# One layer's running maximum spread with 128-row operands, and one list sum moved between two products

## The chip, the core and the metric

The kernel runs on one core of a Trainium2 chip. Its metric is the device time of one execution in microseconds (us); a lower time is better. Below, TensorE is the matrix engine (PE in the rows, PEld for its weight loads), VectorE is DVE, ScalarE is ACT, GpSimd is POOL and SyncE is SP. In the rows TensorE's granted clock is a fraction of full speed: 1.00 is the level of 2.4 GHz, 0.50 that of 1.2 GHz.

## What is computed

Eight sequences of 512 tokens with 256 features, in float32, go through two layers. Cut to what matters:

```
x = x + mlstm(layernorm(x), ctx, ctx)      # 4 heads; decay matrix D = exp(log_D - running max), normalised
x = x + mlp(layernorm(x))                  # 256 -> 1024 -> 256, gelu
x = x + attention(layernorm(x), ctx, ctx)  # 16 heads of 64, softmax
x = x + moe(layernorm(x))                  # 8 experts, 512 places each; h = gelu(x w1.T), y = h w2.T, weighted
```

In the mLSTM each row of the decay matrix is `exp(g[key] - max over keys so far of g)`, where `g` is the input gate less the summed log of the forget gate. In the experts' layer each expert takes its best 512 tokens of those routed to it, and its results, weighted, are added into the output.

## The kernel before, in words

The work is written as a row of stages; inside a stage each engine has its own program, in an order written out by hand, and semaphores join them.

**Gates.** Tokens and context are loaded, normalised and turned, and the gates of all 32 pairs of head and sequence come out as 32 rows of 512. VectorE's program begins with `memset` of the gate weights and two copies that fill `pick` (L308 to L310), then waits for the first tokens (L311). At the end it splits the running maximum `gmax` into a high and a low part and writes them to `ghl`, rows 0 to 31 and 32 to 63 (L353, L354). `pick` has 64 rows of 32 columns: the unit matrix twice.

**Mixer and MLP** (`mix_and_mlp`). A step `b` runs from -2 to 8 and does the mixer of sequence `b + 2`, the MLP of sequence `b`, and the turns between them. For each head `spread_max` (L465) multiplies a column of `pick`, broadcast to 128 columns, with `ghl`: every partition of the result in PSUM then holds the running maximum of that head, 512 columns wide. ScalarE makes `Dm = exp(...)` of it (L576). The other products of TensorE in a step are `states` (L475), `spread_decay` (L483, 64 rows), `scores` (L492, 64 rows), `values` (L504, L507), `turn` (L434), `hidden` (L446) and `mapped` (L456). In the steps -2 and -1 there is no MLP yet.

**Attention** and the **router** follow; the change touches neither.

**Experts** (`experts`). For each expert VectorE builds a one-hot table and the numbers to be summed (`build`, L1588 to L1603), TensorE sums them (`sum_numbers`, L1517, 32 small matmuls), and VectorE turns the sums into the lists of rows to fetch and to write (`read`, L1613 to L1621; the list to fetch is `idx_get`, L1618). GpSimd then issues four indirect transfers that gather the expert's tokens (`gather`, L1483), and later four that add the results into the output (`put`, L1494). GpSimd's order is: gathers of experts 0, 1 and 2; then for each expert its puts and the gathers of the expert three further on. TensorE's order for each expert is: turn the tokens (L1528), first product in two halves `f = 0` and `f = 1` (L1536), the list sum of the expert two further on, second product (L1546). ScalarE applies gelu to each half (L1579); VectorE scales the results into `y` (L1637), and after expert `e` builds and reads the list of expert `e + 3`.

```
                for e in range(AHEAD):
                    build(e)
                    read(e)
                for e in range(E):
                    scale(e)
                    if there(e + AHEAD):
                        build(e + AHEAD)
                        read(e + AHEAD)
```

Of the kernel before, what the change touches and what calls it, by code (L numbers as in the profile page):

```python
# [11 lines left out]
F32 = mybir.dt.float32  # L12
F32R = mybir.dt.float32r
# [3 lines left out]
ALU = mybir.AluOpType  # L17
# [4 lines left out]
P = 128  # L22
B, S, D = 8, 512, 256
# [3 lines left out]
DC = D // P  # L27
MH, MD = 4, 64
# [13 lines left out]
KINDS = 2 * TPB + 6  # L42
# [124 lines left out]
def mlstm_gates(nc, c, x, x_all, xnT_all, ctxT_all, g, ctx_in, ig_kernel, ig_bias, fg_kernel, fg_bias, prefetch):  # L167

    R = MH * B
    WIDE = 2 * R + R - MH  # L170
    RING = 4
    with ExitStack() as ctx:
# [10 lines left out]
        ps = ctx.enter_context(nc.psum_tensor("mg_ps", [P, 8, 512], F32))  # L183
# [5 lines left out]
        ident = c["ident"]  # L189

        with nc.Block() as block:
# [114 lines left out]
            @block.vector  # L306
            def _(dve):
                dve.memset(gate_w[:, :, :], 0.0).then_inc(s["gw"], 1)  # L308
                dve.tensor_copy(g["pick"][0:R, :], ident[0:R, 0:R])
                dve.tensor_copy(g["pick"][R:2 * R, :], ident[R:2 * R, R:2 * R])  # L310
                dve.wait_ge(s["x0"], 16)  # L311
                norm_stats_dve(dve, s, 0, x_all, tmp[0])
                dve.wait_ge(s["gw"], 1)
                dve.wait_ge(s["w"], 16 * 2)
                for half in range(2):
                    src = gk_in[:, :, MH * half:MH * half + MH]
                    at = R - MH + R * half
                    dst = gate_w[:, :, at:at + MH]
                    dve.tensor_copy(dst[:, 0:DC, :], src[:, 0:DC, :]).then_inc(s["gw"], 1)

                    dve.tensor_tensor(dst[:, DC:2 * DC, :], src[:, DC:2 * DC, :], src[:, 2 * DC:3 * DC, :],
                                      ALU.add).then_inc(s["gw"], 1)
                for i in range(B):
                    if i + 1 < B:
                        dve.wait_ge(s[f"x{(i + 1) % RING}"], 16 * ((i + 1) // RING + 1))
                        if i:
                            wait_apart(dve, s["xn"], i)
                        norm_stats_dve(dve, s, i + 1, x_all, tmp[(i + 1) % 2])
                    norm_apply_dve(dve, s, i, x_all, tmp[i % 2],
                                   lambda: dve.wait_ge(s["xn_turned"], i - 1) if i > 1 else None)  # L330

                def row(ins, k):
                    ins.then_inc(s["rows"], 1)
                    dve.wait_ge(s["rows"], k)

                dve.wait_ge(s["fg"], 1)
                dve.tensor_tensor(fg[:, :], ps[3 * R:4 * R, GATE_BANK, :], fg[:, :], ALU.add).then_inc(s["summed"], 1)
                dve.wait_ge(s["summed"], 1)
                row(dve.scalar_tensor_tensor(out=absf[:, :], in0=fg[:, :], scalar=-1.0, in1=fg[:, :],
                                             op0=ALU.mult, op1=ALU.max), 1)  # L340
                dve.wait_ge(s["act_rows"], 2)
                row(dve.scalar_tensor_tensor(out=fg[:, :], in0=fg[:, :], scalar=0.0, in1=lfg[:, :],
                                             op0=ALU.min, op1=ALU.subtract), 2)
                row(dve.tensor_tensor_scan(cums[:, :], c["ones_row"][0:R, :], fg[:, :], 0.0, ALU.mult, ALU.add), 3)
                dve.wait_ge(s["ig"], 1)
                dve.tensor_tensor(ig[:, :], ps[2 * R:3 * R, GATE_BANK, :], ig[:, :], ALU.add).then_inc(s["summed"], 1)
                dve.wait_ge(s["summed"], 2)
                row(dve.tensor_tensor(gg[:, :], ig[:, :], cums[:, :], ALU.subtract), 4)
                row(dve.tensor_tensor_scan(gmax[:, :], gg[:, :], gg[:, :], -3.0e38, ALU.max, ALU.max), 5)
                row(dve.tensor_scalar(neg_r[:, :], gmax[:, :].rearrange("r (t p) -> r t p", p=P)[:, :, P - 1],  # L350
                                      -1.0, None, ALU.mult), 6)
                row(dve.tensor_tensor(logmax[:, :], cums[:, :], gmax[:, :], ALU.add), 7)
                row(dve.tensor_copy(g["ghl"][0:R, :], gmax[:, :]), 8)  # L353
                row(dve.tensor_tensor(g["ghl"][R:2 * R, :], gmax[:, :], g["ghl"][0:R, :], ALU.subtract), 9)  # L354
                dve.wait_ge(s["act_rows"], 6)
                row(dve.tensor_copy(g["bhl"][0:R, :], bb[:, 0:S - P]), 10)
                row(dve.tensor_tensor(g["bhl"][R:2 * R, :], bb[:, 0:S - P], g["bhl"][0:R, :], ALU.subtract), 11)
                dve.wait_ge(s["cols_ps"], 1)
                dve.tensor_copy(g["cols"][:, :, :], ps[:, COL_BANK, 0:KINDS * R].rearrange("p (k r) -> p k r", r=R)
                                ).then_inc(s["cols"], 1)  # L360
# [17 lines left out]
def mix_and_mlp(nc, c, g, x_all, xnT_all, ctxT_all, ctx_in, early, prefetch):  # L378

    R = MH * B  # L380
# [5 lines left out]
    with ExitStack() as ctx:  # L386
# [17 lines left out]
        H_BANK, Y_BANK, OUT_BANK = 0, 4, 6  # L404
# [14 lines left out]
        with nc.Block() as block:  # L419
# [9 lines left out]
            def _(pe):  # L429
# [32 lines left out]
                def spread_max(m, h):  # L462
                    wait_count(pe, s["exp"], MH * m + h)
                    r = MH * m + h
                    pe.matmul(ps[:, G_BANK, :], g["pick"][:, r:r + 1].broadcast_to([2 * R, P]), g["ghl"][:, :],  # L465
                              start=True, stop=True).then_inc(s["g_ps"], 1)

                def states(m, p):
# [976 lines left out]
def experts(nc, c, landed, rows, out, w1T, w2T, chunk, slot_b):  # L1445
# [4 lines left out]
    with ExitStack() as ctx:  # L1450
# [20 lines left out]
        def there(e):  # L1471
            return e < E
# [4 lines left out]
        with nc.Block() as block:  # L1477
# [32 lines left out]
            @block.tensor  # L1510
            def _(pe):
                def sum_numbers(e):
                    pe.wait_ge(s["built"], e + 1)
                    if e:
                        pe.wait_ge(s["lists"], e)
                    for t in range(NT):
                        ins = pe.matmul(ps[:, SLOT_BANK, 0:3 * CT], onehot[:, e % 2, t, :],  # L1517
                                        number[:, e % 2, t, :, :].rearrange("p a c -> p (a c)"), start=t == 0,
                                        stop=t == NT - 1)
                    ins.then_inc(s["slot_ps"], 1)  # L1520

                def turn_tokens(e):
                    got(pe, e)
                    if e:
                        pe.wait_ge(s["xT"], e)
                    for k in range(DC):
                        for t in range(CT):
                            ins = pe.transpose(ps[:, X_BANK + k, P * t:P * t + P], xg[:, e, t, P * k:P * k + P],  # L1528
                                               c["ident"][:, :])
                    ins.then_inc(s["x_ps"], 1)  # L1530

                def hidden(e):
                    pe.wait_ge(s["xT"], e + 1)
                    for f in range(EC):
                        for k in range(DC):
                            ins = pe.matmul(ps[:, H_BANK + f, :], w1T[:, e, k, P * f:P * f + P], xT[:, e % 2, k, :],  # L1536
                                            start=k == 0, stop=k == DC - 1)
                        ins.then_inc(s["h_ps"], 1)

                def mapped(e):  # L1540
                    pe.wait_ge(s["hT"], EC * (e + 1))
                    for t in range(CT):
                        if e:
                            pe.wait_ge(s["y"], CT * (e - 1) + 2 * (t // 2) + 2)
                        for f in range(EC):
                            ins = pe.matmul(ps[:, Y_BANK + t // 2, D * (t % 2):D * (t % 2) + D],  # L1546
                                            hT[:, f, P * t:P * t + P], w2T[:, e, f, :], start=f == 0,
                                            stop=f == EC - 1)
                        if t % 2:
                            ins.then_inc(s["y_ps"], 1)  # L1550

                sum_numbers(0)
                sum_numbers(1)
                turn_tokens(0)
                for e in range(E):
                    hidden(e)
                    if there(e + 2):
                        sum_numbers(e + 2)
                    mapped(e)
                    if there(e + 1):  # L1560
                        turn_tokens(e + 1)
# [90 lines left out]
def build(nc, a, rows, out):  # L1652
    with ExitStack() as ctx:
# [8 lines left out]
        with ExitStack() as mid:  # L1662
# [4 lines left out]
                     "loaded": mid.enter_context(nc.semaphore("m_loaded"))}  # L1667
            with ExitStack() as mix:
                sbx = allocator(mix, nc, "mx")
                g = {"cols": sbx("cols", [P, KINDS, MH * B], F32), "ghl": sbx("ghl", [2 * MH * B, S], F32R),  # L1670
                     "bhl": sbx("bhl", [2 * MH * B, S - P], F32R), "pick": sbx("pick", [2 * MH * B, MH * B], F32R)}
                early = {"w1": sbx("w1", [P, DC, F], F32), "w2": sbx("w2", [P, FC, D], F32),
                         "b1": sbx("b1", [P, FC], F32), "b2": sbx("b2", [P, D], F32),
                         "after": sbx("after", [P, D], F32), "w_row": sbx("w_row", [P, D], F32),
# [54 lines left out]
```

## Time and profile before

| | us |
|---|---|
| three runs | 1875.43, 1878.68, 1882.32 |
| median of the runs | 1878.68 |
| the profiled execution, its own time | 1875.32 |
| its span, first to last instruction | 1873.6 |

All rows below are from the profiled execution, and their times count from the start of its span. Its own time lies 1.7 us above its span and 3.4 us below the median of the runs. A row of a timeline gives the start, the time that the merged group took, engine, line, operation, what it writes and reads, how many instructions, and in brackets how long the engine was idle before and what ended that.

### The profile page before, as it was taken

The numbers are of one execution on the slowest core, as the hardware profiler recorded it, in microseconds if no ns is written. First come the engines' busy times: TensorE is split into PE (matmuls) and PEld (weight loads), VectorE is DVE, ScalarE is ACT, GpSimd is POOL, SyncE is SP. The second block draws the span as 40 slices with busy tenths as digits, with TensorE's granted clock in tenths as the row PEclk, the third lists the DMA queues.
The fourth block names the chain that finished last, engine by engine and source line by source line (L and its number), as shares of the span: only waits on it lengthen the run. The fifth ranks groups of instructions, "written<-read, shape, count | busy, mean of one in ns | idle before, by whom it ended". The sixth has DMA issues, their size and how long they took to land. (4 is left out here: it accounts for less than half of the span.)

```text
span 1873.6 us, 26058 instructions
## 1 busy us (share of the span) xinstructions
PE 1695.3 (90%) x8890; PEld 1150.4 (61%) x8890; DVE 1191.2 (64%) x2640; ACT 842.8 (45%) x1870; POOL 620.0 (33%) x746
## 2 busy tenths in 40 slices
PE   6469999997999999999999999999999999873574
PEld 4356777774566666666666666666666666572352
DVE  5443445441677777777777777777777777567761
ACT  3323433332555555555555555555555555421110
POOL 2143444441232323323333332323333233210385
PEclk9659999998999999999999999999999999955797
DMA  7100000003222232322223232232322223144154
GB/s 256 20 17 18 12 12 1 1 1 102 49 67 60 54 68 45 68 51 63 64 50 68 46 68 56 58 68 46 68 48 66 61 53 68 23 143 132 40 87 57
DMA packets 66657, 109.46 MB, mean 58 GB/s; under 512 B 16088, under 2 KB 48096, under 8 KB 66528
## 3 DMA queue, kind: packets, MB, share of 16 engines
q1 hardware_dynamic: 60384, 99.29, 21.5%
q0 software_dynamic: 6144, 8.52, 2.9%
q8 instruction: 72, 1.18, 0.3%
q14 instruction: 57, 0.47, 0.1%
HBM read 27.84 MB, written 12.85 MB: 22 GB/s over the span
## 5 line engine op out<-in xcount | busy, mean ns | idle before, releaser
L1028 POOL TENSOR_SCALAR at_Pr<-at_Pr,at_rinv 128x512 f32<-128x512 f32 x512 | 354.1, 692 | 825.4 <-DVE at_rinv L1055 825.4
L1007 ACT ACTIVATE at_Pr<-at_ps,at_nmax 128x512 f32<-128x512 f32 x512 | 352.0, 687 | 522.5 <-DVE at_nmax L1050 520.9
L1050 DVE TENSOR_REDUCE at_nmax<-at_ps 128x1 f32<-128x512 f32 x512 | 350.9, 685 | 138.3 <-PE at_ps L915 127.3
L915 PE MATMUL at_ps<-at_k,at_q 128*128 128x512 f32 x1024 | 420.0, 491 | 9.3 <-DMA at_k<-at_k_own 7.6
L926 PE MATMUL at_ps<-k_ident,at_Pr 128*128 128x128 f32 x2048 | 310.5, 274 | 4.3 <-POOL at_Pr L1028 4.3
L926 PEld LDWEIGHTS at_ps<-k_ident,at_Pr 128*128 128x128 f32 x2048 | 249.5, 140 | 93.6 <-POOL at_Pr L1028 33.1
L1062 DVE COPY at_PT<-at_ps 128x512 f32<-128x512 f32 x384 | 261.3, 681 | 0.0
L915 PEld LDWEIGHTS at_ps<-at_k,at_q 128*128 128x128 f32 x1024 | 174.3, 190 | 128.6 <-issue 119.2
L936 PE MATMUL at_ps<-at_PT,at_V 128*64 128x512 f32 x1024 | 235.5, 602 | 0.9 <-DVE at_PT L1062 0.9
L1055 DVE RECIPROCAL at_rinv<-at_rsum 128x1 f32<-128x1 f32 x512 | 83.3, 163 | 174.5 <-ACT at_Pr L1007 172.5
L936 PEld LDWEIGHTS at_ps<-at_PT,at_V 128*64 128x64 f32 x1024 | 68.1, 137 | 122.7 <-issue 121.6
L946 PE MATMUL at_ps<-at_wo,at_oT 128*128 128x256 f32 x512 | 131.6, 380 | 0.8 <-ACT at_oT L993 0.8
L456 PE MATMUL mm_ps<-mx_w,mm_hT 128*128 128x256 f32 x512 | 120.9, 382 | 0.0
L446 PE MATMUL mm_ps<-m_xnT,mx_w 128*128 128x512 f32 x256 | 112.7, 598 | 1.3 <-ACT m_xnT L599 1.3
L903 PE MATMUL at_ps<-at_w_rest,m_ctxT 128*128 128x128 f32 x896 | 109.2, 275 | 0.0
L894 PE MATMUL at_ps<-m_xnT,at_w_rest 128*128 128x512 f32 x224 | 106.4, 598 | 0.0
L894 PE MATMUL at_ps<-m_ctxT,at_w_rest 128*128 128x512 f32 x224 | 105.4, 593 | 0.0
L903 PEld LDWEIGHTS at_ps<-at_w_rest,m_ctxT 128*128 128x128 f32 x896 | 104.5, 192 | 0.0
L456 PEld LDWEIGHTS mm_ps<-mx_w,mm_hT 128*128 128x128 f32 x512 | 93.7, 190 | 16.6 <-issue 5.3
L1037 DVE SCALAR_TENSOR_TENSOR at_q<-at_ps,m_b_all,at_q 64x512 fp32r<-64x512 f32 x128 | 96.0, 750 | 8.6 <-ACT at_q L976 5.7
L1007 ACT ACTIVATION_READ_ACCUMULATOR at_Pr<-at_ps,at_nmax 128x1 f32 x512 | 98.7, 193 | 0.0
L946 PEld LDWEIGHTS at_ps<-at_wo,at_oT 128*128 128x128 f32 x512 | 87.4, 190 | 8.3 <-ACT at_oT L993 1.7
(235 smaller groups left out, 2026.3 us busy)
## 6 DMA issues: line engine op xcount, KB each, us to landing
at_k<-at_k_own SPq DMA_DIRECT2D x256, 256.0 KB, 4.2
k_x<-in_x SPq DMA_DIRECT2D x8, 512.0 KB, 7.8
mg_ctx<-in_ctx SPq DMA_DIRECT2D x8, 512.0 KB, 7.8
mx_ctxn<-in_ctx SPq DMA_DIRECT2D x8, 512.0 KB, 3.9
rows<-lo_xn SPq DMA_DIRECT2D x8, 512.0 KB, 3.0
out<-k_x SPq DMA_DIRECT2D x1, 4096.0 KB, 14.6
r_w<-in_L_ffn_w SPq DMA_DIRECT2D x16, 256.0 KB, 5.8
mx_w<-in_L_ffn_w SPq DMA_DIRECT2D x2, 1024.0 KB, 10.5
```

The costliest lines, as they stand in the source:

```text
L446: ins = pe.matmul(ps[:, H_BANK + f % 4, :], w1_s[:, k, P * f:P * f + P], xnT_all[:, k, b * S:b * S + S], start=k == 0, stop=k == DC - 1)
L456: ins = pe.matmul(ps[:, Y_BANK + t // 2, D * (t % 2):D * (t % 2) + D], hT[:, f, P * t:P * t + P], w2_s[:, f, :], start=f == 0, stop=f == F ...
L894: ins = pe.matmul(ps[:, A_BANK + k, :], weights(k, d, hp), src[:, d, b * S:b * S + S], start=d == 0, stop=d == DC - 1)
L903: ins = pe.matmul(ps[:, A_BANK, P * t:P * t + P], ctxT_all[:, d, b * S + P * t:b * S + P * t + P], weights(2, d, hp), start=d == 0, stop=d ...
L915: ins = pe.matmul(ps[:, S_BANK + j % 2, :], q2[:, u % 2, h, q:q + P], k2[:, u % 2, h, part, :], start=part == 0, stop=part == 1)
L926: ins = pe.transpose(ps[:, T_BANK + j % 2, P * t:P * t + P], Pr[:, j % 4, P * t:P * t + P], c["ident"][:, :])
L936: ins = pe.matmul(ps[AD * h:AD * h + AD, O_BANK, :], V[:, u % 2, t, AD * h:AD * h + AD], PT[:, u % 2, h, t, :], start=t == 0, stop=t == TP ...
L946: ins = pe.matmul(ps[:, Y_BANK - half, D * (t % 2):D * (t % 2) + D], oT[:, P * t:P * t + P], wo_s[:, u % HP, :], start=True, stop=True)
L1007: act.activation(Pr[:, j % 4, :], ps[:, S_BANK + j % 2, :], ACT.Exp, bias=nmax[:, j % 4:j % 4 + 1], accum_out=rsum[:, j % 4:j % 4 + 1]).th ...
L1028: pool.tensor_scalar(Pr[:, n % 4, :], Pr[:, n % 4, :], rinv[:, n % 4:n % 4 + 1], 1.0, ALU.mult, ALU.mult).then_inc(s["pn"], 1)
L1050: dve.tensor_reduce(nmax[:, j % 4:j % 4 + 1], ps[:, S_BANK + j % 2, :], AX.X, ALU.max, negate=True).then_inc(s["nmax"], 1)
L1062: dve.tensor_copy(PT[:, u % 2, j // TPB, :, q:q + P], ps[:, T_BANK + j % 2, :].rearrange("p (t q) -> p t q", t=TPB)).then_inc(s["pt_v"], 1)
```

## The change

Two edits that don't depend on each other. The first gives `ghl` and `pick` 128 rows instead of 64, fills the new rows with zeros in two VectorE instructions ahead of the wait for the first tokens, and broadcasts the column of `pick` over 128 rows, so that each of the 32 matmuls of `spread_max` has 128 rows in both operands. The second splits the first product of an expert into its halves and, for expert 0 alone, puts the sum of list 2 between them; for the other experts the order stays.

```
+                dve.tensor_scalar(g["pick"][2 * R:P, :], ident[2 * R:P, 0:R], 0.0, None, ALU.mult)
+                dve.tensor_scalar(g["ghl"][2 * R:P, :], c["ones_row"][2 * R:P, :], 0.0, None, ALU.mult)
                 dve.wait_ge(s["x0"], 16)
...
-                    pe.matmul(ps[:, G_BANK, :], g["pick"][:, r:r + 1].broadcast_to([2 * R, P]), g["ghl"][:, :],
+                    pe.matmul(ps[:, G_BANK, :], g["pick"][:, r:r + 1].broadcast_to([P, P]), g["ghl"][:, :],
                               start=True, stop=True).then_inc(s["g_ps"], 1)
...
-                def hidden(e):
+                def hidden(e, f):
                     pe.wait_ge(s["xT"], e + 1)
-                    for f in range(EC):
-                        for k in range(DC):
-                            ins = pe.matmul(ps[:, H_BANK + f, :], w1T[:, e, k, P * f:P * f + P], xT[:, e % 2, k, :],
-                                            start=k == 0, stop=k == DC - 1)
-                        ins.then_inc(s["h_ps"], 1)
+                    for k in range(DC):
+                        ins = pe.matmul(ps[:, H_BANK + f, :], w1T[:, e, k, P * f:P * f + P], xT[:, e % 2, k, :],
+                                        start=k == 0, stop=k == DC - 1)
+                    ins.then_inc(s["h_ps"], 1)
...
                 for e in range(E):
-                    hidden(e)
-                    if there(e + 2):
+                    hidden(e, 0)
+                    if e == 0:
+                        sum_numbers(2)
+                    hidden(e, 1)
+                    if e and there(e + 2):
                         sum_numbers(e + 2)
                     mapped(e)
...
-                g = {"cols": sbx("cols", [P, KINDS, MH * B], F32), "ghl": sbx("ghl", [2 * MH * B, S], F32R),
-                     "bhl": sbx("bhl", [2 * MH * B, S - P], F32R), "pick": sbx("pick", [2 * MH * B, MH * B], F32R)}
+                g = {"cols": sbx("cols", [P, KINDS, MH * B], F32), "ghl": sbx("ghl", [P, S], F32R),
+                     "bhl": sbx("bhl", [2 * MH * B, S - P], F32R), "pick": sbx("pick", [P, MH * B], F32R)}
```

## Rows read from the trace of the kernel before

**Rows 1.** The page: clock in 40 slices, and the attention's score product, mean in ns.
```profile
PEclk9659999998999999999999999999999999955797
...
L915 PE MATMUL at_ps<-at_k,at_q 128*128 128x512 f32 x1024 | 420.0, 491 | 9.3 <-DMA at_k<-at_k_own 7.6
```
**Rows 2.** Busy time by stretch: length, PE, PEld, DVE, ACT, POOL, clock, DMA share, GB/s.
```profile
79.46:82.03 2.57, 2.57 (x23) 2.50 (x23) 0.00 (x0) 0.79 (x4) 0.64 (x1) 1.00 0.01 3
...
111.17:116.04 4.87, 4.87 (x22) 4.75 (x22) 1.46 (x4) 0.49 (x2) 0.69 (x1) 0.50 0.00 0
116.04:119.73 3.69, 3.69 (x14) 2.95 (x13) 0.00 (x0) 1.79 (x6) 1.59 (x2) 0.50 0.00 0
...
134.00:136.00 2.00, 2.00 (x5) 0.99 (x4) 1.93 (x3) 0.37 (x1) 0.56 (x1) 0.74 0.00 0
...
140.00:421.00 281.00, 281.00 (x1412) 198.80 (x1411) 124.00 (x301) 108.44 (x220) 125.92 (x107) 1.00 0.03 8
```
**Rows 3.** Timeline of POOL in the experts' stage.
```profile
1762.47 0.95 POOL L1483 DMA_INDIRECT ex_xg<-rows,ex_idx_get  x1 [0.30 <-issue]
1770.05 0.94 POOL L1483 DMA_INDIRECT ex_xg<-rows,ex_idx_get  x1 [6.64 <-DVE ex_idx_get L1618]
...
1775.06 1.63 POOL L1494 DMA_INDIRECT out<-ex_y,ex_idx_put  x1 [0.30 <-issue]
...
1782.58 1.02 POOL L1483 DMA_INDIRECT ex_xg<-rows,ex_idx_get  x1 [0.30 <-issue]
...
1864.18 1.56 POOL L1494 DMA_INDIRECT out<-ex_y,ex_idx_put  x1 [0.30 <-issue]
```
**Rows 4.** Timeline of DVE in the gates' stage.
```profile
8.27 1.41 DVE L58 BATCH_NORM_STATS2 mg_stats<-k_x 128x6 f32<-128x256 f32 x4 [3.27 <-DMA k_x<-in_x]
...
61.34 0.68 DVE L354 TENSOR_TENSOR mx_ghl<-mg_gmax,mx_ghl 32x512 fp32r<-32x512 f32 x1
```
**Rows 5.** The line of `spread_max`: ns min/median/max, first and last start.
```profile
L465 PE MATMUL mm_ps<-mx_ghl,mx_pick x32: 472/494/792, 70.0 to 373.4; 64*128 64x512 f32 x32
```
**Rows 6.** Timeline of PE in the mixer's first two steps.
```profile
84.72 1.32 PE L492 MATMUL mm_ps<-m_xnT,m_ctxT 64*128 64x128 f32 x16
...
120.40 2.38 PE L492 MATMUL mm_ps<-m_xnT,m_ctxT 64*128 64x128 f32 x16
...
129.01 1.91 PE L434 MATMUL mm_ps<-k_ident,mm_xn 128*128 128x128 f32 x8
132.18 10.24 PE L446 MATMUL mm_ps<-m_xnT,mx_w 128*128 128x512 f32 x20 [1.25 <-ACT m_xnT L599]
```
**Rows 7.** Timeline of PE in the experts' stage (the second row from a narrower window).
```profile
1761.82 6.06 PE L1536 MATMUL ex_ps<-ex_xT,k_w1T 128*128 128x512 f32 x8 [1.16 <-ACT ex_xT L1570]
...
1765.39 1.63 PE L1536 MATMUL ex_ps<-ex_xT,k_w1T 128*128 128x512 f32 x2
...
1767.72 0.95 PE L1517 MATMUL ex_ps<-ex_number,ex_onehot 128*128 128x12 bf16 x32
1768.57 3.72 PE L1546 MATMUL ex_ps<-k_w2T,ex_hT 128*128 128x256 f32 x16
...
1836.87 3.72 PE L1546 MATMUL ex_ps<-k_w2T,ex_hT 128*128 128x256 f32 x16 [0.69 <-ACT ex_hT L1579]
```
**Rows 8.** Timeline of DVE in the experts' stage.
```profile
1763.45 0.22 DVE L1603 CAST ex_number<-ex_is_chunk 128x128 bf16<-128x128 f32 x1
...
1769.11 0.17 DVE L1618 CAST ex_idx_get<-ex_tok 128x4 int32<-128x4 f32 x1
...
1770.67 0.88 DVE L1637 TENSOR_SCALAR ex_y<-ex_ps,ex_sc 128x256 f32<-128x256 f32 x2 [0.67 <-PE ex_ps L1546]
...
1773.12 0.28 DVE L1588 TENSOR_TENSOR ex_is_chunk<-k_slot,k_token_chunk 128x128 f32<-128x128 f32 x1
...
1780.66 0.17 DVE L1618 CAST ex_idx_get<-ex_tok 128x4 int32<-128x4 f32 x1
```
**Rows 9.** Busy time by stretch, columns as in rows 2: half a us of the first product.
```profile
1766.50:1767.00 0.50, 0.50 (x2) 0.22 (x2) 0.00 (x0) 0.00 (x0) 0.00 (x0) 0.89 0.00 0
```

## The prediction

> **What bounds the kernel now.** I read four views in this order. First the page, for where the clock is low: most slices are at 9, and the low ones (6, 5; 5, 5, 7) lie at the start, where the change's first edit acts, and near the end, where its second acts [rows 1]. Second the busy time by stretch: from 140 to 421 us TensorE is busy all the time at clock 1.00 [rows 2]. So the mixer is bound by TensorE from its step 0 on, and a microsecond by which that step starts earlier is a microsecond of the whole. Before it, in the steps -2 and -1, TensorE works in pieces, and two of these, 111.17 to 116.04 and 116.04 to 119.73, were busy throughout at clock 0.50 [rows 2]. Third, GpSimd's timeline in the experts' stage: gather 2 began at 1770.05 after 6.64 us of idleness that the list of expert 2 ended. After that the shown transfers stand 0.30 us apart, the last, at 1864.18, included [rows 3]; it is the last instruction of the span but for waiting on its landing. So this stage hangs on GpSimd's queue of gathers and puts, with TensorE off its path. Fourth, the timelines of TensorE and VectorE there, for what sets the lists.
>
> **The zeros.** Two VectorE instructions are added, 64 rows by 32 columns and 64 by 512. The nearest row is the 512-column instruction that writes the same tile, 0.68 us [rows 4]; I take 0.7 for the large one and at most as much for the small, 1.4 us together. Lower bound: nothing. They stand ahead of a wait for the first tokens, in which VectorE sat idle for 3.27 us [rows 4]. That hides them whole; without that cover they would cost 1.4 us. Cost: 0.
>
> **The 32 matmuls.** With 64 rows the median is 494 ns, at 512 columns [rows 5]. The attention's product with 128 rows and as many columns has a mean of 491 ns [rows 1]. The duration doesn't depend on the rows. Direct cost: 0.
>
> **What the rows may do to the clock.** Here the trace gives no direct answer, since no row shows this matmul with 128 rows, so I bound it from both sides. What rows show is that being busy is not enough: TensorE was busy for 4.87 of 4.87 us and then 3.69 of 3.69 at 0.50 [rows 2]. The first stretch is `values`, with 65 and 130 columns a matmul; the second is one `spread_max` of 64 rows and `states`. In step 0 the first product, 512 columns and 128 rows, begins at 132.18 [rows 6], and the clock rises during it: a mean of 0.74 over 134 to 136 puts the rise at 135.04, since 1.04 us at 0.50 and 0.96 at 1.00 give it [rows 2]. [...] It could be the columns alone (the change gives nothing), or the rows too (one more full matmul beside `states` could tip the clock at some 118 us).
>
> By the Trainium skill, page "TensorE: Matmul & The Clock Gate", section "What's actually happening", the clock is released by how busy the engine has recently been. The trace does not agree: 8.56 us of unbroken business at 0.50 [rows 2]. By that rule nothing changes here, for the engine is exactly as busy with 64 rows as with 128.
>
> The price, if the clock rose at 118 and stayed up until 135.04: the rest of `states`, 119.73 less 118 is 1.73 us, and half of it is saved, 0.87. `scores`, 2.38 against 1.32 at full clock: 1.06 [rows 6]. The four parts of `values` after it: the same work took 4.87 at half and 2.57 at full clock, 2.30 [rows 2]. The turn, 1.91 [rows 6]: half, 0.95. The first product up to 135.04, 2.86 us: half, 1.43. Sum 6.6 us, all ahead of a stage that TensorE bounds. Bounds: 0 to 6.6. I take 0, because no row shows that rows count, and because the price needs the clock to stay up through the waits between these pieces.
>
> **The list sum.** Call the halves of expert 0's first product H0 and H1, the sum S, the second product M. H0 and H1 are eight records; the fifth, the first of H1, starts at 1765.39. Then S at 1767.72, M at 1768.57 [rows 7]. The numbers that S adds were ready at 1763.45 + 0.22 = 1763.67 [rows 8], before H0 ends, so in its new place S waits for nothing, and H1 behind it doesn't either.
>
> S starts at 1765.39 instead of 1767.72: 2.33 us earlier. From S to the first gather 1770.05 - 1767.72 = 2.33 us went by [rows 3, 7], by way of VectorE's `read`, where it waited for S alone. So gather 2 can issue at 1767.72 and everything behind it on GpSimd could come up to 2.33 earlier: the four gathers, then put 0 at 1775.06 - 2.33 = 1772.73, then gather 3 at 1782.58 - 2.33 = 1780.25 [rows 3]. GpSimd also waits for the output's initial copy after gather 2; in the trace it goes on after 0.30 us, so that wait has long been met.
>
> What is late next? H1 follows S after 0.85 us (S to M [rows 7]), so it starts at 1766.24. The clock is 0.50 until 1766.61 (a mean of 0.89 over the half microsecond from 1766.50 [rows 9]: 0.11 us at the low level). H1's work, in full-clock time, is (1766.61 - 1765.39)/2 + (1767.72 - 1766.61) = 1.72. Started at 1766.24, with the same rise, it does 0.19 before it and needs 1.53 after: end 1768.14. Then M must wait for the gelu of H1, which S used to cover; for expert 6, which has no S, that wait was 0.69 us [rows 7]. M starts at 1768.83, 0.26 later than before. This delay, call it d, goes on: VectorE's first scaling 1770.67 + 0.26 = 1770.93 plus at most 0.88 is ready before put 0 wants it at 1772.73. But the build of list 3 follows the scaling, 1773.12 + d, and its list comes at 1780.66 + d [rows 8]. From a list to its gather takes 1770.05 - 1769.11 = 0.94. So gather 3 can start at 1781.60 + d, where it started at 1782.58. The gain is therefore not 2.33 but 0.98 - d: with d = 0.26, **0.7 us**. From there on GpSimd has no gap and I carry the 0.7 to the end; the two waits for landings at the end move along with it.
>
> The second wait for `xT` in `hidden` has been met by then; it costs nothing. For experts 1 to 7 the order is what it was.
>
> **Sum.** 0 + 0 + 0 - 0.7 = -0.7 us: the profiled execution's span goes from 1873.6 to 1872.9, its own time from 1875.32 to 1874.6. It lies 3.4 us below the median; against that median the forecast is 1878.0.
>
> **Rivals.**
> (a) Rows count for the clock, and the head of the mixer runs at full clock from some 118 us: -6.6 and -0.7 give 1871.4. For it: two busy stretches at 0.50, one of them with the 64-row matmul in it. Against: nothing separates rows from columns, and only one such matmul lies there. A part of it (the clock up for one or two pieces) gives about -3: 1875.
> (b) Slower: S between H0 and H1 breaks the run of wide matmuls, and the clock doesn't rise at 1766.61. H1 then takes 2 x 1.72 = 3.44, ends at 1769.68, M starts at 1770.37, d = 1.80, and gather 3 is 0.82 late: 1879.5. It decides from d = 0.98 on. If M too is at half clock, another 3.7 us [rows 7] come on top: +4.5, 1883.2. For it: S is 32 matmuls of 12 columns [rows 7]. Against: S is short beside H0, and H0 has been at work for 3.57 us by then.
> (c) Gather 3 is held by something that moves with none of this, and nothing is gained: 1878.7.
>
> **How the numbers follow.** Forecast 1878.0: 0.50. (a) whole 0.16, in part 0.11. (b) 0.15, of which 0.05 with M. (c) 0.08. What a measurement of this kernel tells from no change is about 0.3%, 5.6 us; its runs lie 6.9 us apart. Faster by more than that is (a) whole and a little of the spread: 0.17. Slower by more needs (b) with M, and the spread of the runs on top: 0.05. The rest, 0.78, is within 0.3%. The range goes down to (a) whole, 1871.5, and up to half-way into the worse (b), with the runs' own spread: 1882.5.
>
> **What would show it.** Right: the two zeroing instructions end before 8.27; L465 has 128 rows and a median near 494 ns; gather 2 issues near 1767.7 by the clock of this trace and gather 3 about 0.7 earlier, bounded by the list, with a gap on GpSimd of about 1.6 us before it (1781.87 less 1780.25). Wrong: clock 1.00 somewhere between 111 and 132 us (rival a), or 0.50 all through H1 (rival b), or a gap on GpSimd of over 2.3 us before gather 3.

## The result and the profile after

The changed kernel took 1861.02 us (median of 4 runs, 1860.35 to 1861.19) against 1877.07 for the kernel before (4 runs, 1875.43 to 1882.32): a ratio of 0.9899, 95% interval 0.9885 to 0.9913. It is 16 us faster, where 0.7 were forecast, and 1861.0 lies below the forecast range, 1871.5 to 1882.5. The profiled execution took 1861.19 us, its span is 1859.5, so 14.1 us less than the span before.

Where did they go? A line's own view gives the start of its first and its last instruction, and four such starts cut the span into pieces: the first `spread_max`, the first `hidden` of the MLP, the last `mapped` of the MLP, and the first list sum of the experts. The pieces, in us:

```
                     before   after   difference
to the first spread    70.0    70.5     +0.5
head: to the MLP       62.2    59.9     -2.3
MLP with mixer        311.3   300.6    -10.7
attention, router    1305.4  1305.0     -0.4
experts               124.7   123.5     -1.2
```

So three quarters lie in a stretch where TensorE is busy all the time before and after, at clock 1.00 but for its first microseconds [rows 2]. It does the same work in less time. Its timeline shows where; the first rows are of the kernel before, in steady state:

```profile
230.96 1.89 PE L456 MATMUL mm_ps<-mx_w,mm_hT 128*128 128x256 f32 x8
232.78 0.49 PE L465 MATMUL mm_ps<-mx_ghl,mx_pick 64*128 64x512 f32 x1
233.21 1.61 PE L475 MATMUL mm_ps<-mm_vaug,mm_kw 128*128 128x130 f32 x12
234.65 1.89 PE L456 MATMUL mm_ps<-mx_w,mm_hT 128*128 128x256 f32 x8
236.47 0.50 PE L465 MATMUL mm_ps<-mx_ghl,mx_pick 64*128 64x512 f32 x1
236.90 1.99 PE L456 MATMUL mm_ps<-mx_w,mm_hT 128*128 128x256 f32 x8
238.82 0.44 PE L483 MATMUL mm_ps<-mx_bhl,mm_pick_half 64*128 64x384 f32 x1
```

The same place in the changed kernel (two lines further down in the code):

```profile
224.67 1.89 PE L458 MATMUL mm_ps<-mx_w,mm_hT 128*128 128x256 f32 x8
226.21 0.58 PE L467 MATMUL mm_ps<-mx_ghl,mx_pick 128*128 128x512 f32 x1
226.63 1.50 PE L477 MATMUL mm_ps<-mm_vaug,mm_kw 128*128 128x130 f32 x12
227.97 1.89 PE L458 MATMUL mm_ps<-mx_w,mm_hT 128*128 128x256 f32 x8
229.51 0.58 PE L467 MATMUL mm_ps<-mx_ghl,mx_pick 128*128 128x512 f32 x1
229.92 1.89 PE L458 MATMUL mm_ps<-mx_w,mm_hT 128*128 128x256 f32 x8
231.74 0.44 PE L485 MATMUL mm_ps<-mx_bhl,mm_pick_half 64*128 64x384 f32 x1
```

Read the starts, not the durations. From the start of the eight `mapped` matmuls to that of `spread_max`: 1.82 us before, 1.54 after. The record of `spread_max` itself got longer, 0.49 to 0.58, while its place in the row got shorter. What follows it is faster too: `states` to the next `mapped` 1.44 and 1.34, the eight `mapped` after the second spread 1.92 and 1.82. The whole stretch shown: 7.86 and 7.07 us, 0.79 for two spreads, 0.40 each. And `spread_decay`, which kept its 64 rows, still comes 1.82 after the eight `mapped` before it.

The weight loads show where it goes. First the kernel before, then the changed one, TensorE's load timeline at the same place; in brackets is how long no load ran (gaps under 0.15 us are not printed):

```profile
230.97 1.49 PEld L456 LDWEIGHTS mm_ps<-mx_w,mm_hT 128*128 128x128 f32 x7 [0.24 <-issue]
232.78 0.18 PEld L465 LDWEIGHTS mm_ps<-mx_ghl,mx_pick 64*128 64x128 f32 x1 [0.33 <-issue]
233.20 1.42 PEld L475 LDWEIGHTS mm_ps<-mm_vaug,mm_kw 128*128 128x128 f32 x12 [0.24 <-issue]
```

```profile
224.67 1.49 PEld L458 LDWEIGHTS mm_ps<-mx_w,mm_hT 128*128 128x128 f32 x7 [0.24 <-issue]
226.18 0.19 PEld L467 LDWEIGHTS mm_ps<-mx_ghl,mx_pick 128*128 128x128 f32 x1
226.40 1.54 PEld L477 LDWEIGHTS mm_ps<-mm_vaug,mm_kw 128*128 128x128 f32 x12
```

Compare each load with its own matmul. With 64 rows neither goes ahead: the spread's load starts with its matmul (232.78 and 232.78), 0.33 us behind the last load of `mapped`, and that of `states` with its own (233.20 and 233.21), 0.24 us behind the spread's. With 128 rows both follow the load before them within 0.03 us, while earlier matmuls still run, and the load of `states` is 0.23 us ahead of its matmul (226.40 and 226.63). The gap of 0.24 in the first row of both kernels is no such wait: that load follows matmuls of 128 rows and 512 columns that start 0.43 us apart, and a load of 0.19 us leaves 0.24 between. The Trainium skill, page "TensorE: Matmul & The Clock Gate", section "The mechanism", says in its list of what overlaps that a load overlaps with matmuls in flight only when the row groups differ; a few lines above, the same section also lets a load go ahead that targets a background weight buffer. The trace does not agree with the first as it stands: full rows behind full rows load ahead, and the loads that wait stand where the rows change between 128 and 64. No run shows which buffer a load went to.

The sum was there to be read in the kernel before. The line view of `spread_max`, from which the prediction took the durations [rows 5], goes on with what the engine waited for, and the changed kernel's answers to it:

```profile
  issue: 14.9, 27
```

```profile
L467 PE MATMUL mm_ps<-mx_ghl,mx_pick x32: 479/582/780, 70.5 to 361.0; 128*128 128x512 f32 x32
...
  issue: 6.4, 1
```

6.4 us in one piece are the same in both (the idle time ahead of the first one). The other 8.5 us, in 26 pieces of 0.33, are gone. Of these 26, 24 lie beside the MLP, one for each spread there: `wide_in_head` below, with 64 rows beside the MLP alone, keeps 24 pieces, 8.0 us. In the head there were two.

The experts' stage, which answers to [rows 3], [rows 7] and [rows 8], GpSimd, TensorE and VectorE:

```profile
1754.69 0.94 POOL L1485 DMA_INDIRECT ex_xg<-rows,ex_idx_get  x1 [4.19 <-DVE ex_idx_get L1622]
...
1768.24 1.02 POOL L1485 DMA_INDIRECT ex_xg<-rows,ex_idx_get  x1 [1.33 <-DVE ex_idx_get L1622]
...
1849.93 1.56 POOL L1496 DMA_INDIRECT out<-ex_y,ex_idx_put  x1 [0.30 <-issue]
```

```profile
1748.68 3.78 PE L1537 MATMUL ex_ps<-ex_xT,k_w1T 128*128 128x512 f32 x4 [1.16 <-ACT ex_xT L1574]
1752.26 1.05 PE L1519 MATMUL ex_ps<-ex_number,ex_onehot 128*128 128x12 bf16 x32
1753.16 2.23 PE L1537 MATMUL ex_ps<-ex_xT,k_w1T 128*128 128x512 f32 x4
1756.08 3.72 PE L1547 MATMUL ex_ps<-k_w2T,ex_hT 128*128 128x256 f32 x16 [0.69 <-ACT ex_hT L1583]
```

```profile
1766.83 0.17 DVE L1617 COPY ex_sums<-ex_ps 128x12 f32<-128x12 f32 x1 [1.05 <-PE ex_ps L1519]
...
1767.23 0.17 DVE L1622 CAST ex_idx_get<-ex_tok 128x4 int32<-128x4 f32 x1
```

Counted from the start of the first product, S came at 3.58 us instead of 5.90, M at 7.40 instead of 6.75, and gather 3 at 19.56 instead of 20.76: GpSimd now has a gap of 1.33 us there, ended by the list.

### The profile page after: what moved, and what is told of

The parts are those of the page before. It is cut to its first block and busy times, and to the rows that moved or that the text cites. A ratio compares the mean times of both kernels' runs of the same rounds, so it can differ in the third digit from the quotient of the medians.

```text
span 1859.5 us, 26060 instructions
## 1 busy us (share of the span) xinstructions
PE 1683.3 (91%) x8890; PEld 1152.6 (62%) x8890; DVE 1192.0 (64%) x2642; ACT 842.8 (45%) x1870; POOL 619.9 (33%) x746
```

## The experiments

The kernels were timed in four groups, each beside the kernel before on the same chip: `rows_only`, `sum_only`, `rows96` and `beside64` beside 1880.58 us; `after_again`, `rows65`, `decay128` and `all128` beside 1879.21; `sums_scalar` and `list3_early` beside 1880.48; `wide_beside_mlp` and `wide_in_head` beside 1880.09. `after_again` is the changed kernel once more. Because heads and the attention differ by some us from run to run, I read each kernel's profile by the pieces as well, all taken as above (the first row is the profiled execution of the kernel before; that of the changed kernel stands in the table above):

```
kernel            rows of the spread      median   head    MLP   experts
before            64                                62.2  311.3  124.7
sum_only          64                     1877.84    65.5  309.9  123.4
beside64          64                     1880.22    63.6  307.5  124.8
sums_scalar       64                     1879.82    65.4  309.9  125.8
wide_beside_mlp   64 in the head, 128    1868.89    66.6  302.4  124.9
wide_in_head      128 in the head, 64    1871.44    60.0  310.0  123.2
rows_only         128                    1866.73    60.0  302.0  124.2
rows96            96                     1863.57    64.1  300.6  123.3
rows65            65                     1863.88    59.5  300.6  123.0
after_again       128                    1859.97    56.3  300.6  123.1
decay128          128, decay too         1866.73    61.5  300.7  125.1
all128            128, all               1868.18    57.6  306.9  123.5
list3_early       128                    1865.99    60.4  302.3  124.0
```

**The two edits apart.** `rows_only` puts the list sum back behind the second half for all experts:

```
-                    hidden(e, 0)
-                    if e == 0:
-                        sum_numbers(2)
-                    hidden(e, 1)
-                    if e and there(e + 2):
+                    hidden(e, 0)
+                    hidden(e, 1)
+                    if there(e + 2):
                         sum_numbers(e + 2)
```

> The first edit alone (128 rows in the operands of the running maximum; the list sum stays where it was). Theory A: TensorE loads the weights of a matmul while the one before it still runs only if both use the same rows of the array; each of the 32 matmuls with 64 rows therefore cost a wait when entering it (0.28 us by the spacing of starts) and a smaller one when leaving it (about 0.1 us), 32 x 0.4 = 12.8 us at most, and this edit alone brings 11 to 13 us: 1864 to 1866. Rival B (the rows only raised the clock ahead of step 0): 2 to 3 us, 1874 to 1875.

1866.73 us, ratio 0.9924 (0.9907 to 0.9941): 14 us less than before (11 to 17.5 by the interval), somewhat more than the 12.8 that theory A gave as the most, and far from rival B. By the pieces 9.3 us of it are the waits beside the MLP; what the head adds is taken up further down. `sum_only` takes out the zeros and the 128 rows and keeps the list sum's place:

```
-                dve.tensor_scalar(g["pick"][2 * R:P, :], ident[2 * R:P, 0:R], 0.0, None, ALU.mult)
-                dve.tensor_scalar(g["ghl"][2 * R:P, :], c["ones_row"][2 * R:P, :], 0.0, None, ALU.mult)
...
-                    pe.matmul(ps[:, G_BANK, :], g["pick"][:, r:r + 1].broadcast_to([P, P]), g["ghl"][:, :],
+                    pe.matmul(ps[:, G_BANK, :], g["pick"][:, r:r + 1].broadcast_to([2 * R, P]), g["ghl"][:, :],
```

> The second edit alone (the sum of list 2 between the halves of the first product of expert 0; the running maximum keeps 64 rows). Theory A and the two traces: from gather 0 to the last put 1.3 us less, so 1875 to 1876 and hard to tell from before. Rival: the edits only pay together, or this one brings most of the 16 us: 1861 to 1870.

1877.84, ratio 0.9988 (0.9978 to 0.9998), the experts' piece 123.4. The first edit brings nearly everything, the second about a microsecond: over all profiles the experts' piece is 124.9 us on average in the four with the list sum in its old place (124.2 to 125.8) and 123.7 in the nine with the new place and nothing else moved there (123.0 to 125.1, so the two groups overlap).

**How many rows must it be?** `rows96` and `rows65` fill and use 96 and 65 rows instead of 128, as here:

```
-                    pe.matmul(ps[:, G_BANK, :], g["pick"][:, r:r + 1].broadcast_to([P, P]), g["ghl"][:, :],
+                    pe.matmul(ps[:, G_BANK, :], g["pick"][:, r:r + 1].broadcast_to([3 * R, P]), g["ghl"][:, :],
```

> As the changed kernel, but the operands of the running maximum have 96 rows, the third 32 filled with zeros. Theory A: 96 rows are still another set than the 128 of the neighbours, so the weights still wait: only the list sum's 1 to 2 us are gained, 1875 to 1876, and the spacing from the eight matmuls before it stays at 1.82 us. Rival C (the cost goes with the number of missing rows): half of the gain, about 1868, and a spacing near 1.68.

1863.57 us, ratio 0.9897 (0.9878 to 0.9917), MLP piece 300.6. Theory A as it was put fell: 96 rows are another set than 128, and still nothing waits. Rival C fell with it, for the gain is whole. What was left was a coarser form, that more than 64 rows take the same part of the array as 128 do.

> As the changed kernel, but the operands of the running maximum have 65 rows, one more than before the change. Theory A in the form that 96 rows left standing (64 rows take half of the array's rows, more than 64 take all of them, and weights go ahead only between matmuls that take the same part): as fast as with 128 rows, MLP steps of 300.6 us from the first product to the last, spacing 1.54 us. Rival C (the number of rows counts): close to the kernel before, 311 us and 1.82.

1863.88 us, ratio 0.9930 (0.9904 to 0.9956), MLP piece 300.6. TensorE's timeline with 65 rows:

```profile
227.23 1.89 PE L458 MATMUL mm_ps<-mx_w,mm_hT 128*128 128x256 f32 x8
228.77 0.58 PE L467 MATMUL mm_ps<-mx_ghl,mx_pick 65*128 65x512 f32 x1
```

Starts 1.54 us apart, as with 128. One row more than 64 is enough; the count of rows beyond that does nothing.

**Is it the matmul or its neighbours?** `beside64` is the kernel before with one line moved, so that three groups with 64 rows stand together:

```
-                    if mix:
-                        spread_max(m, 1)
                     if mlp:
                         mapped(b, 1, 0)
                     if mix:
+                        spread_max(m, 1)
                         spread_decay(m, 0)
```

> The kernel before, all with 64 rows, but the second running maximum of each sequence stands right ahead of the two other matmul groups with 64 rows (spread of the decay, scores) instead of eight matmuls with 128 rows earlier. Theory A: for the six sequences that run beside an MLP one entry and one exit fall away, 6 x 0.4 = 2.4 us less: 1874 to 1875. Rival D (a 64-row matmul is slow by itself, whatever stands beside it): no change, 1877, or a little slower since ScalarE gets it later.

1880.22 us, ratio 0.9994 (0.9984 to 1.0003): the time as a whole can't tell, 2.4 us lie within its interval. The MLP piece can: 307.5 against 309.9 in `sum_only` and `sums_scalar`, which run this stretch in the old order and, like it, with the clock up from its start: 2.4 us less. Its timeline:

```profile
233.46 3.62 PE L456 MATMUL mm_ps<-mx_w,mm_hT 128*128 128x256 f32 x16
237.00 0.49 PE L465 MATMUL mm_ps<-mx_ghl,mx_pick 64*128 64x512 f32 x1
237.02 0.48 PE L492 MATMUL mm_ps<-m_xnT,m_ctxT 64*128 64x128 f32 x2
237.34 0.33 PE L483 MATMUL mm_ps<-mx_bhl,mm_pick_half 64*128 64x384 f32 x1
237.51 1.05 PE L492 MATMUL mm_ps<-m_xnT,m_ctxT 64*128 64x128 f32 x14
238.49 1.99 PE L456 MATMUL mm_ps<-mx_w,mm_hT 128*128 128x256 f32 x8
```

From the `mapped` in front to the `mapped` behind: 5.03 us. In the kernel before the same work, with its spread apart, takes 5.43 (from 234.65 above to what follows the scores, which take 1.26 us from 238.82 on). The matmul with 64 rows is not slow by itself; going in and out is. Its neighbours there include scores that lie in the other 64 rows, and no gap is printed between their loads either: here the change between 128 and 64 costs, not which 64 they are.

`decay128` gives the spread of the decay 128 rows as well, on top of the changed kernel:

```
+                dve.tensor_scalar(g["bhl"][2 * R:P, :], c["ones_row"][2 * R:P, 0:S - P], 0.0, None, ALU.mult)
...
-        pick_half = sb("pick_half", [2 * R, R, MD], F32R)
+        pick_half = sb("pick_half", [P, R, MD], F32R)
...
+                dve.tensor_scalar(pick_half[2 * R:P, :, :].rearrange("k r a -> k (r a)").rearrange(
+                    "k (n f) -> k n f", f=S), c["ones_row"][2 * R:P, :].rearrange("p (a f) -> p a f", a=1).broadcast_to(
+                        [2 * R, R * MD // S, S]), 0.0, None, ALU.mult).then_inc(s["own"], 1)
```

> The changed kernel, and the spread of the decay has 128 rows too (64 of them zeros). It stands between eight matmuls of 128 rows and the scores with 64. Theory A: the change of rows, and its wait, only moves from the entry of the decay to the entry of the scores: within 1 us of the changed kernel. Rival D (each matmul with 64 rows costs by itself, whatever stands beside it): 16 x 0.4 = 6 us less, about 1855.

```profile
232.24 1.89 PE L459 MATMUL mm_ps<-mx_w,mm_hT 128*128 128x256 f32 x8
233.78 0.52 PE L486 MATMUL mm_ps<-mx_bhl,mm_pick_half 128*128 128x384 f32 x1
234.23 1.16 PE L495 MATMUL mm_ps<-m_xnT,m_ctxT 64*128 64x128 f32 x16
235.32 1.99 PE L459 MATMUL mm_ps<-mx_w,mm_hT 128*128 128x256 f32 x8
```

The decay now comes 1.54 us after `mapped`, and the scores wait instead (their first load begins 0.29 us after the decay's has ended): from `mapped` to `mapped` 3.08 us, 3.09 in the changed kernel (229.92 to 233.01). MLP piece 300.7. The wait moved, as theory A said, and rival D fell. For the whole the expectation (within 1 us) failed: it took 1866.73 us, 6.8 more than the changed kernel in the same group. In the two profiles 1.3 of it lie ahead of the first spread (71.2 instead of 69.9 us), where the added zeros run, 5.2 in the head, where `after_again` has the shortest of all, and 2.0 in the experts' stage; why the last two differ stays open.

`all128` widens the scores too:

```
-                            ins = pe.matmul(ps[:, S_BANK + h, P * t:P * t + P], ctxT_all[own_h, p, at],
-                                            xnT_all[own_h, p, at], start=True, stop=True)
+                            ins = pe.matmul(ps[:, S_BANK + h, P * t:P * t + P], ctxT_all[:, p, at],
+                                            xnT_all[:, p, at], start=True, stop=True)
```

> As the one before, and the scores read 128 rows as well: each head's scores are the sum over both heads of the pair, so that part of the result is another one. No matmul with 64 rows is left in the mixer. Theory A: 16 changes of rows fall away, up to 16 x 0.4 = 6 us less than the changed kernel, 1855, less what the scores of two heads lose by no longer lying in different halves of the array. Rival: that loss eats all of it: 1861 or more.

```profile
231.01 1.89 PE L459 MATMUL mm_ps<-mx_w,mm_hT 128*128 128x256 f32 x8
232.55 0.53 PE L486 MATMUL mm_ps<-mx_bhl,mm_pick_half 128*128 128x384 f32 x1
232.92 1.95 PE L495 MATMUL mm_ps<-m_xnT,m_ctxT 128*128 128x128 f32 x16
234.70 1.89 PE L459 MATMUL mm_ps<-mx_w,mm_hT 128*128 128x256 f32 x8
```

No wait is left, and yet the stretch takes 3.69 us instead of 3.09, and the MLP piece 306.9 instead of 300.6. The scores themselves take 1.78 us from their start to the next `mapped`, with 64 rows 1.26: the two heads of a pair, in different halves of the array, had run side by side. In the kernel before, two scores start together at 239.44 us and the next two 0.11 later; with 128 rows they come one by one, 0.11 apart. The rival held: that is worth more than the wait.

**The head and the MLP apart.** `wide_beside_mlp`, and with the condition reversed `wide_in_head`:

```
+                    n = P if m >= 2 else 2 * R
+                    pe.matmul(ps[:, G_BANK, :], g["pick"][0:n, r:r + 1].broadcast_to([n, P]), g["ghl"][0:n, :],
```

> The changed kernel, but the running maximum of the first two sequences, whose mixer runs ahead of the MLP, is spread with 64 rows as before; the other 24 of the 32 matmuls have 128. Theory A (waits at changes of rows): from the first product of the MLP to the last 300.6 to 302 us, as in the changed kernel; the head before it, from the first spread on, 62 to 65 us as in the kernels with 64 rows; 1863 to 1866 in all. Rival B (a higher clock in the head brings a large part): 1870 or more.

> The reverse: only the 8 matmuls of the first two sequences have 128 rows, the other 24 have 64. Theory A: the MLP stretch stays at 309.9 to 311.3 us, the head is shorter by 8 x 0.4 to 0.5 = 3 to 4 us (56 to 61 us); with the list sum 1871 to 1875 in all. If the waits were all and the clock had no part, the low level of the clock would last as long in the head as with 64 rows everywhere; if it rises near 120 us as in the profile of the changed kernel, the clock takes part of the head's gain.

1868.89 us, ratio 0.9949 (0.9937 to 0.9961), and 1871.44, ratio 0.9960 (0.9947 to 0.9973). Each is faster than before, and the pieces fall where the wide matmuls are: MLP 302.4 and 310.0, head 66.6 and 60.0. The expectation for the first one's whole was 3 to 6 us too low, since its head was long and its first product still ran at half clock; that of the second held. The clock has a part in the head: over the ten runs each, the granted clock of the whole span was 0.940 to 0.944 with 128 rows there (0.942 on average) and 0.936 to 0.941 with 64 (0.938). It is not seen in every group: `rows65` averaged 0.9405 over its four runs, the kernel before beside it 0.940. Busy time by stretch over the head, `wide_beside_mlp` first:

```profile
70.00:132.00 62.00, 42.12 (x206) 36.80 (x206) 22.75 (x42) 12.06 (x39) 19.46 (x19) 0.56 0.06 18
```

```profile
70.00:132.00 62.00, 40.39 (x226) 35.34 (x226) 23.84 (x47) 14.88 (x45) 22.51 (x22) 0.67 0.06 18
```

A mean clock of 0.56 with 64 rows there, 0.67 with 128. 65 rows gave a head of 59.5 us as well; why the clock was up for longer stays open. The five heads with 64 rows took 62.2 to 66.6 us, the seven with more rows in the spreads there and nothing else changed in it 56.3 to 64.1: 64.7 and 60.0 on average. The waits can be at most 8 x 0.39 = 3.1 of these 4.7 us, and rather less: only two gaps of the loads lie in the head, and in the changed kernel the spread of the decay then waits 0.23 us for VectorE at 76.79 and again at 104.63, which it didn't before. By its ratio `wide_in_head` is 7.5 us faster (5.1 to 10.0); less 1.2 for the list sum and at most 3.1 for the waits, an estimated 3 us (1 to 6) are left, and the clock is the only other difference that I found.

**The list sum.** In four traces the copy that reads a list's sums out of PSUM started 0.03 to 0.04 us after the sum's end as long as GpSimd issued no put. When it did, the copy came mostly 0 to 0.3 us before a put's end, once 0.1 after it, with VectorE idle until then. So it was for list 3 before: the sum ended at 1779.29. The two rows, VectorE's and GpSimd's:

```profile
1780.26 0.17 DVE L1613 COPY ex_sums<-ex_ps 128x12 f32<-128x12 f32 x1 [1.99 <-PE ex_ps L1517]
```

```profile
1778.86 1.55 POOL L1494 DMA_INDIRECT out<-ex_y,ex_idx_put  x1 [0.30 <-issue]
```

0.97 us late, and in the changed kernel 0.03, where the sum ended at 1766.80. A put was running there too, from 1765.36 to 1766.91: the sum happened to end just before the put did. `sums_scalar` tries another instruction in the kernel before:

```
-                    dve.tensor_copy(sums[:, :, :], ps[:, SLOT_BANK, 0:3 * CT].rearrange("p (a k) -> p a k", a=3)
-                                    ).then_inc(s["lists"], 1)
+                    dve.tensor_scalar(sums[:, :, :], ps[:, SLOT_BANK, 0:3 * CT].rearrange("p (a k) -> p a k", a=3),
+                                      1.0, None, ALU.mult).then_inc(s["lists"], 1)
```

> The kernel before, but VectorE reads the list sums out of PSUM with a multiplication by 1.0 instead of a copy. In four traces this copy came 0.03 to 0.04 us after the sum when GpSimd was issuing no put, and only some 0.1 us before a put's end when it was (0.97 us late for list 3 before). Theory E (that kind of copy is held by GpSimd's put): late by 0.04 us for every list, list 3 and its gather 0.9 us earlier, 0.9 us less between the first list sum and the end. Rival F (whatever VectorE does first after this wait is held, or the sum itself ends later than shown): late as before.

1879.82, ratio 1.0000 (0.9988 to 1.0011). List 3 was late by 0.88 us, the later ones by 1.30 to 3.55: theory E fell. The kind of instruction doesn't matter; what holds the list stays open.

`list3_early` goes after the gap of 1.33 us that the changed kernel has ahead of gather 3:

```
                 for e in range(E):
+                    if e == 0:
+                        build(AHEAD)
                     scale(e)
...
                     mapped(e)
+                    if e == 0:
+                        sum_numbers(3)
```

(and the build and the sum of list 3 fall away from their old places).

> The changed kernel, and list 3 as well comes earlier: VectorE builds its table before it scales the results of expert 0, in the 3.5 us in which it waits for them, and TensorE sums it right behind the second product of expert 0. In the changed kernel GpSimd waited 1.33 us for list 3. If that wait is what is left of the list sum's 2.4 us, it goes to 0, put 0 comes some 0.4 us later, and the stretch from the first list sum to the end gets 0.9 us shorter than 123.1 to 123.5. If the next list, or a result that a put wants, holds GpSimd instead, nothing is gained.

```profile
1766.62 1.63 POOL L1496 DMA_INDIRECT out<-ex_y,ex_idx_put  x1 [1.77 <-DVE ex_y L1643]
...
1774.14 1.02 POOL L1485 DMA_INDIRECT ex_xg<-rows,ex_idx_get  x1 [0.30 <-issue]
```

The gap ahead of gather 3 is gone, and one of 1.77 us ahead of put 0 has come, where 0.4 were expected: VectorE scales only after it has built. The experts' piece is 124.0 instead of the 0.9 less that were expected, the whole 1865.99 us, not better than the changed kernel, 1859.97 in its own group:

> The changed kernel once more, beside the next three on the same chip: 1860 to 1863.

No version that I ran beats the changed kernel.

## Why the prediction was wrong

Step by step, as it was put.

**What bounds the kernel** was right: TensorE from step 0 of the mixer on, GpSimd's queue in the experts' stage. A microsecond saved on TensorE there was a microsecond of the whole.

**The zeros** cost nothing: they took 0.18 and 0.42 us, the second from 5.10 on, and the first statistics began at 8.21.

**"The 32 matmuls ... The duration doesn't depend on the rows. Direct cost: 0"** is the step that failed. It read the cost of a matmul off the duration of its record. With 128 rows that record even got longer, a median of 582 ns where 494 was forecast, while the stretch got shorter. The spacing of starts in the kernel before had the difference: the attention's product of [rows 1] follows a matmul of 128 rows at 0.03 us (600.48 and 600.51), `spread_max` follows its last `mapped` at 0.31 (232.48 and 232.78). With 64 rows between neighbours of 128, a spread cost 0.28 us on the way in and some 0.12 on the way out. Over the 24 spreads beside the MLP that is 9.3 us at full clock: 309.9 less 300.6, 0.39 each. Another 1.4 us of the 10.7 is the clock: before, the first product ran at half speed from 132.18 to 135.04 [rows 2, 6], in the changed kernel the clock was up before that product began. That need not be the edit's doing: with 64 rows too `sum_only`, `beside64` and `sums_scalar` had it up by then (309.9 and less), and with 128 rows beside the MLP `rows_only`, `wide_beside_mlp` and `list3_early` had not (302.0 to 302.4).

**What the rows may do to the clock** was the wrong question for most of the gain. Rival (a) put -6.6 us on it. The clock did rise in the head, at 118.7 us in the changed kernel (0.77 on average from 118.5 to 119.0), but fell back before `values`, and the head as a whole became 2.3 us shorter, its waits included. A clock of 1.00 between 111 and 132 us was the sign given for rival (a), and it doesn't tell the rows: from 120 to 125 us the granted clock averaged 0.63 in `sum_only`, 0.56 in `sums_scalar` and 0.84 in `beside64`, all with 64 rows, against 0.50 in the kernel before. `sum_only` does the same work there as the kernel before, so one profile can't tell what makes the clock rise. Still, with wide spreads in the head alone some 3 us are left to the clock, so rival (a) was not empty, but it was neither the main gain nor priced from a row of it. The step asked for the clock alone and left out the gaps between matmuls, which is what the first edit acts on.

**The list sum** was right in its mechanism, and sized too small: 0.7 forecast, 1.2 in the two profiles. S came 2.32 us earlier (2.33 forecast), and gather 3 waits for list 3, as was said. M was 0.65 us later, not 0.26: H1 took 2.23 us from its start, where I had worked out 1.90, and S 0.05 more. What made up for it is the term that was missing, the copy of list 3's sums, late by 0.97 us before and by 0.03 now: 0.97 - 0.03 - 0.65 is 0.3, and with the 0.98 less 0.07 that the gather was behind its list, 1.2. That the copy came on time for this list is luck as far as the runs tell, since in the changed kernel the next two came 0.95 and 1.23 late. The gap ahead of gather 3 was 1.33 us, 1.6 forecast.

**The rivals.** (b) didn't happen: the clock rose 0.55 us after H1 began (at 1753.71, by a mean of 0.79 from 1753.5 to 1754.0; 0.37 worked out). None of them held the direct cost of a change of rows, and the range was built from them alone, so it could not reach 1861.

## What to carry to other kernels

On a saturated TensorE cost a matmul by the spacing of starts, from its predecessor to its successor, and look at the load's idle time: a matmul that takes 64 rows between matmuls that take 128 pays on the way in and out, 0.39 us together here (fewer than 64 were not tried). Zero rows that fill it up to 65, 96 or 128 took no time there, but where two narrow matmuls run side by side in different halves of the array, as the scores do, leave them narrow. An edit that widens one of two narrow neighbours only moves the wait to the other.

## What the runs showed of the hardware that was not expected

- In the changed kernel a weight load behind matmuls with the same 128 rows goes ahead while they run (0.23 us ahead of its own matmul at 226.40); from 128 to 64 rows it waits 0.33 us, and on the way back 0.24. 65, 96 and 128 rows behave alike (1.54 us of spacing each), 64 don't (1.82).
- Two heads' scores with 64 rows in different halves take 1.26 us where the same sixteen records with 128 rows take 1.78.
- A list's sums are read up to 3.6 us late when GpSimd issues puts around the sum's end, whether VectorE copies or multiplies. Its cause is open.
